# Order of transposes and matmuls on TensorE in the attention of a graph network's encoder

## The chip, the cores and the metric

One core of a Trainium2 chip. The metric is the device time of one execution in microseconds (us); less is better. The kernel runs four graph layers one after the other; the change lies in one stage of the fourth.

## The reference, cut to what matters

There are 2708 nodes with 512 features and a dense adjacency matrix. The stage in question is the attention of the fourth layer's encoder, with four heads of 128 features:

```
Xw  = einsum('hnd,hde->hne', Xh, W)                  # 4 heads x 2708 x 128
sig = sigmoid(f1[:, :, None] + f2[:, None, :])
att = masked_softmax(pattern * sig, pattern != 0)    # both patterns are adj
Xa  = einsum('hij,hjd->hid', att, Xw)
Xn  = batchnorm(Xa as 2708 x 512); then an MLP, and a decoder that uses att again
```

## The kernel before, in words

Rows are padded to 22 tiles of 128. The stage works in **units**: unit u is one tile of 128 rows for one head. There are 88 units (`UNITS`); `place` (L1116) gives each its row tile, head and side r, so that units 2n and 2n+1 are the two row tiles of the same head. Such a pair is called pair n here (44 of them); one output of the attention is made for each pair.

What a unit goes through, and on which engine:

- `score(u)` (L1214, ScalarE): sigmoid of a 128x2708 row block into the buffer `slot(u)` (L1220). There are five such buffers; before it overwrites one, it waits until all transposes of the unit that used it last are done (`before`, L1124: four units back for three of four units, else eight).
- `weigh(u)` (L1267, VectorE): product with the adjacency rows and the row maximum (L1273).
- GpSimd: the negated maximum `nm` (L1203).
- `expo(u)` (L1223, ScalarE): exp with row sums, in place (L1225). Its end lets the transposes of unit u begin (`p_ready`).
- `turn_group(u, g)` (L1334, TensorE): 22 transposes in six groups g = 0 to 5 (four tiles each, two in the last), each group into one of five PSUM banks that are used in turn (`ring`, L1113). Each transpose is one instruction at L1342. Group 0 waits for `p_ready`; every group waits until the group five places earlier was copied out.
- the copies of the groups to SBUF tile `pt`: group 2 on ScalarE (`keep`, L1228, row L1232), the others on VectorE (`keep`, L1276, row L1281). `kept` (L1128) gives the semaphore and its count.
- `mul(n, lo, hi)` (L1346, TensorE): of the 22 accumulating matmuls of pair n those from lo to hi; the moving operand is the pair's copied transposes, 256 columns. Each of these matmuls is two instructions at L1354 in the trace.

TensorE's loop (L1366 to L1376) runs over the units and in each over the six groups: the transposes of group g of unit u, then a part of the matmuls of the pair before, n = u//2 - 1. The 11 matmuls that a unit does are spread over its groups as 1, 2, 2, 2, 2, 2. Pair 43 has its matmuls behind the loop (L1376).

ScalarE's order is written out by hand for four units b to b+3 (L1242 to L1262): `expo(b)`, `keep(b-1)`, `expo(b+1)`, `expo(b+2)`, `keep(b)`, `expo(b+3)`, `score(b+4)`, `keep(b+1)`, `score(b+5)`, `score(b+6)`, `keep(b+2)`, `score(b+7)`. A table load stands at each change between exp and sigmoid. Every eighth unit a small row of inverse sums is handled besides (`ri_out`, `inverse`, `turn_ri`).

VectorE copies the groups of unit u in order (all but group 2); behind its group 4 stands `weigh(u+3)`, behind group 0 of an even unit the copy of a finished accumulator, `raw` (L1283).

SyncE stores each copied group of a pair to HBM (L1170). GpSimd also fetches adjacency rows and scales finished outputs (L1195).

Of the kernel before, what the change touches and what calls it, by code (L numbers as in the profile page):

```python
# [49 lines left out]
def wait(eng, sem, value):  # L50

    if isinstance(value, int) and value <= 0:
        return
    eng.wait_ge(sem, value)
# [24 lines left out]
def build(nc, x, adj_rows, adj_cols, adj_tiles, ident, w0, a0_self, a0_neigh, b0, w1, b1, w2a, w2b, a2_w, a2_b,  # L79
# [30 lines left out]
    with top:  # L110
# [87 lines left out]
        with ExitStack() as ph:  # L198
# [15 lines left out]
            with nc.Block() as block:  # L214
                @block.sync
                def _(sp):
                    sp.dma_start(w0_sb[:, :, :], w0).then_inc(w_in, 16)
                    sp.dma_start(vecs[0], a0_self.partition_broadcast(128)).then_inc(vec_in, 16)
                    sp.dma_start(vecs[1], a0_neigh.partition_broadcast(128)).then_inc(vec_in, 16)
                    sp.dma_start(idt[:, :], ident).then_inc(vec_in, 16)  # L220

                    def body(i):
                        for q in (0, 1):
                            j = 2 * i + q
                            wait(sp, turned, j - 1)
                            sp.dma_start(xin[q][:, :], x[j]).then_inc(x_in[q], 16)
                            wait(sp, mask_done, j - 1)
                            sp.dma_start(al[q][:, :], adj_cols[j]).then_inc(adj_in[q], 16)
                    pair_loop(sp, body, first=True)
# [582 lines left out]

        with ExitStack() as ph:
            R, xn, st, xin, xt, _, w_sb = norm_buffers(ph)
            rows = [sb(ph, f"rows{q}", [P, NP]) for q in (0, 1)]
            pr = [sb(ph, f"pr{q}", [P, NP]) for q in (0, 1)]
# [275 lines left out]
        with ExitStack() as ph:  # L1092
# [27 lines left out]
            def slot(u):  # L1120

                return v[u % 4 if u % 4 < 3 else 3 + (u // 4) % 2]
# [5 lines left out]
            def kept(g_index):  # L1128

                u, g = divmod(g_index, NG)  # L1130
                if g == ACT_GROUP:
                    return kept_act, u + 1
                return kept_dve, u * (NG - 1) + g + 1 - int(g > ACT_GROUP)
# [14 lines left out]
            with nc.Block() as block:  # L1148
# [183 lines left out]
                @block.tensor  # L1332
                def _(pe):
                    def turn_group(u, g):  # L1334
                        a, b = GROUPS[g]
                        index = NG * u + g
                        if g == 0:
                            pe.wait_ge(p_ready, u + 1)
                        if index >= len(ring):
                            pe.wait_ge(*kept(index - len(ring)))  # L1340
                        for m in range(a, b):
                            t = pe.transpose(ring[index % len(ring)][:, (m - a) * P:(m - a + 1) * P],  # L1342
                                             slot(u)[:, m * P:(m + 1) * P], idt[:, :])
                        t.then_inc(t_grp, 1)

                    def mul(n, lo, hi):  # L1346
                        h = n % H3
                        for m in range(lo, hi):
                            if m == 0 and n >= 2:
                                pe.wait_ge(xr_ready, n - 1)  # L1350
                            if m % 4 == 0 or m == lo:
                                for r in (0, 1):
                                    pe.wait_ge(*kept(NG * (2 * n + r) + m // 4))
                            t = pe.matmul(acc_t[n % 2][:, 0:P2], HA[:, m, h * D3:(h + 1) * D3],  # L1354
                                          pt[n % 2][:, m, :, :].rearrange("p r n -> p (r n)"),
                                          start=(m == 0), stop=(m == T - 1))
                        if hi == T:
                            t.then_inc(m_done, 1)

                    def turn_ri(p):  # L1360
                        pe.wait_ge(ri_ready, p + 1)
                        wait(pe, ri_row, p)
                        pe.transpose(small[0:2 * H3, 0:P], ri[:, :], idt[:, :]).then_inc(ri_turned, 1)

                    pe.wait_ge(pad_zero, len(v))
                    for u in range(UNITS):  # L1366
                        for g in range(NG):
                            turn_group(u, g)
                            if u == 2 and g == 0:
                                pe.wait_ge(ha_in, 16)  # L1370
                            if u >= 2:
                                base = 11 * (u % 2)
                                mul(u // 2 - 1, base + 11 * g // NG, base + 11 * (g + 1) // NG)
                        if u % 8 == 0 and u > 0:
                            turn_ri(u // 8 - 1)
                    mul(HEADS - 1, 0, T)  # L1376
                    turn_ri(PAIRS - 1)
# [416 lines left out]
```

## Time and profile before

| | |
|---|---|
| Three runs, us | 3789.41, 3787.44, 3789.86 (median 3789.41) |
| Profiled execution, its own time | 3787.66 us |
| Its span from first to last instruction | 3786.1 us |
| TensorE busy over the span | 3400.1 us (90%) |
| VectorE / ScalarE busy | 2330.3 us (62%) / 1679.4 us (44%) |
| Stage of the change | transposes L1342 from 2349.5 us, last matmul L1354 begins 3053.2 us |

Times in the rows are microseconds from the span's start. A busy TensorE includes the modelled ends of pipelined matmuls, so the distance between two starts is the better measure of what an instruction costs it. In a row of a timeline "[1.02 <-ACT pt L1232]" means that the engine had been idle for 1.02 us before this instruction and that the row of ScalarE named there released it. PE is TensorE, PEld its weight loads, DVE VectorE, ACT ScalarE, POOL GpSimd.

### The profile page before, as it was taken

To read this page: it belongs to the slowest core of one execution; us is meant where nothing else is said; L and a number is where in the kernel's file an instruction comes from. 1 tells how busy PE (TensorE), PEld (TensorE's weight loads), DVE (VectorE), ACT (ScalarE), POOL (GpSimd) and SP (SyncE) were. 2 spreads that over 40 slices of the span, in tenths; PEclk is the share of its full clock that TensorE was granted. 3 is DMA by queue.
4 is the path that set the end of the run, shared out by engine and by line. 5 is a ranking of instruction groups with operands and counts; after the bars stand their busy time and mean duration, and the time that the engine had idled before them with its cause. 6 is when DMAs were issued, how large, how long until landed. Compare 5 with 4: busy or idle time off the path is not lost. (4 is left out here: it accounts for less than half of the span.)

```text
span 3786.1 us, 39785 instructions
## 1 busy us (share of the span) xinstructions
PE 3400.1 (90%) x13931; PEld 2134.0 (56%) x13931; DVE 2330.3 (62%) x2850; ACT 1679.4 (44%) x1527; POOL 271.1 (7%) x459
## 2 busy tenths in 40 slices
PE   7899999999978899995999995999999967999995
PEld 4433333333323677773555553877777735888884
DVE  4488888988966455555555553777777734122226
ACT  1288888888852111112222223777777702000002
POOL 1000000000002011110000001000010000000003
PEclk9999999999999999997999997999999989999997
DMA  7500000000012455553222224666666630866653
GB/s 284 179 16 8 15 8 15 16 8 15 8 44 91 189 222 229 218 215 137 79 87 94 94 79 175 233 243 244 244 243 245 231 141 15 369 272 269 273 219 123
DMA packets 109759, 557.51 MB, mean 147 GB/s; under 512 B 14320, under 2 KB 20432, under 8 KB 85584
## 3 DMA queue, kind: packets, MB, share of 16 engines
q1 hardware_dynamic: 88592, 432.35, 30.7%
q0 software_dynamic: 21056, 123.65, 8.5%
q8 instruction: 73, 1.20, 0.1%
q14 instruction: 38, 0.31, 0.0%
HBM read 363.77 MB, written 192.18 MB: 147 GB/s over the span
## 5 line engine op out<-in xcount | busy, mean ns | idle before, releaser
L528 PE MATMUL bank<-dist,hf 128*65 128x512 f32 (+1 forms) x2112 | 860.7, 561 | 63.3 <-ACT dist L491 63.3
L528 PEld LDWEIGHTS bank<-dist,hf 128*65 128x65 f32 x2112 | 277.4, 138 | 637.7 <-issue 489.3
L1354 PE MATMUL bank<-pt,HA 128*128 128x256 f32 x1936 | 505.1, 381 | 3.0 <-DMA HA<-features 3.0
L491 ACT ACTIVATE dist<-dist 128x1408 f32<-128x1408 f32 x352 | 469.2, 1368 | 1.5
L1543 PE MATMUL bank<-w,EM 128*128 128x256 f32 x1936 | 427.0, 381 | 12.7 <-DMA w<-weights 12.7
L993 PE MATMUL bank<-HB,pt 128*128 128x512 f32 x968 | 436.7, 593 | 0.0
L1543 PEld LDWEIGHTS bank<-w,EM 128*128 128x128 f32 x1936 | 369.7, 191 | 63.6 <-DMA w<-weights 12.9
L422 DVE TENSOR_TENSOR dist<-msk,sB 128x1408 f32<-128x1408 uint8 x208 | 337.0, 1620 | 74.7 <-PE bank L528 68.5
L1342 PE MATMUL bank<-idt,v 128*128 128x128 f32 x1936 | 304.4, 278 | 79.5 <-ACT pt L1232 50.7
L482 ACT ACTIVATE dist<-dist,neg_t 128x1408 f32<-128x1408 f32 x208 | 305.2, 1467 | 151.9 <-DVE dist L422 151.9
L1354 PEld LDWEIGHTS bank<-pt,HA 128*128 128x128 f32 x1936 | 328.6, 191 | 26.8 <-DMA HA<-features 3.4
L1281 DVE COPY pt<-bank 128x512 f32<-128x512 f32 (+1 forms) x440 | 265.4, 631 | 105.6 <-PE bank L1342 104.4
L1342 PEld LDWEIGHTS bank<-idt,v 128*128 128x128 f32 x1936 | 242.8, 143 | 149.2 <-ACT pt L1232 67.4
L1273 DVE CUSTOM_DVE_ANT_0 v<-v,rows 128x2708 f32<-128x2708 f32 x88 | 261.4, 2971 | 70.0 <-ACT v L1220 54.7
L164 PE MATMUL bank<-w_sb,xt 128*128 128x512 f32 x528 | 252.6, 622 | 24.4 <-DVE HL L599 11.2
L425 DVE SCALAR_TENSOR_TENSOR dist<-msk,neg_t,sB 128x1408 f32<-128x1408 uint8 x144 | 257.7, 1789 | 24.6 <-PE bank L528 22.0
L993 PEld LDWEIGHTS bank<-HB,pt 128*128 128x128 f32 x968 | 174.2, 191 | 170.2 <-issue 170.2
L146 ACT ACTIVATE xt<-bank 128x512 f32<-128x512 f32 x88 | 52.5, 597 | 484.0 <-PE bank L140 483.2
L1220 ACT ACTIVATE v<-fB,f 128x2708 f32<-128x2708 f32 x88 | 224.1, 2549 | 78.9 <-PE bank L1342 70.9
L1225 ACT ACTIVATE v<-v,nm 128x2708 f32<-128x2708 f32 x88 | 224.1, 2549 | 74.4 <-POOL nm L1203 74.1
L1600 DVE TENSOR_TENSOR at<-bank,riB 128x256 f32<-128x256 f32 x44 | 18.7, 425 | 327.9 <-PE bank L1543 327.9
L699 PE MATMUL bank<-HR,hi 128*128 128x512 f32 x484 | 201.8, 417 | 18.0 <-ACT hi L790 18.0
(161 smaller groups left out, 3684.9 us busy)
## 6 DMA issues: line engine op xcount, KB each, us to landing
w<-weights SPq DMA_DIRECT2D x44, 2816.0 KB, 9.9
weights<-pt SPq DMA_DIRECT2D x220, 512.0 KB, 3.8
al<-in_adj_cols SPq DMA_DIRECT2D x22, 1408.0 KB, 7.5
at<-in_adj_tiles SPq DMA_DIRECT2D x22, 1408.0 KB, 6.7
rows<-in_adj_rows SPq DMA_DIRECT2D x22, 1408.0 KB, 6.8
mrow<-in_adj_rows POOLq DMA_DIRECT2D x22, 1354.0 KB, 8.3
rows_low<-mrow POOLq DMA_DIRECT2D x22, 1354.0 KB, 5.1
rows<-rows_low POOLq DMA_DIRECT2D x22, 1354.0 KB, 8.5
```

Source lines behind the costliest of these rows:

```text
L164: t = pe.matmul(pj[0:P, :], xt[:, k, :], w[:, k, :], start=(k == 0), stop=(k == KT - 1))
L422: dve.tensor_tensor(d[:, :], msk[:, m, c * CW:(c + 1) * CW], sB[hh][:, :], ALU.add).then_inc(d_ready, 1)
L425: dve.scalar_tensor_tensor(out=d[:, :], in0=msk[:, m, c * CW:(c + 1) * CW], scalar=neg_t[0:P, m, bass.ds(hp * 2 + hh, 1)], in1=sB[hh][:, : ...
L482: act.activation(d[:, :], d[:, :], ACT.Square, bias=neg_t[0:P, m, bass.ds(hp * 2 + hh, 1)]).then_inc(sq_act, 1)
L491: act.activation(d[:, :], d[:, :], ACT.Exp, scale=-1.0).then_inc(p_ready, 1)
L528: mm = pe.matmul(sums_bank(hh, k)[0:FW, 0:(b - a) * P], hf[hh][:, m, :], d[:, a * P:b * P], start=(m == 0), stop=(m == T - 1))
L993: t = pe.matmul(acc[q][0:P, :], pt[q][:, m, :], HB[0:P, m, :], start=(m == 0), stop=(m == T - 1))
L1273: dve.tensor_tensor_reduce(s[:, 0:N], s[:, 0:N], rows[r][:, :], 1.0, LOW, ALU.mult, ALU.max, mx[:, u % 16:u % 16 + 1]).then_inc(mx_ready, 1)
L1281: dve.tensor_copy(dst, src).then_inc(kept_dve, 1)
L1342: t = pe.transpose(ring[index % len(ring)][:, (m - a) * P:(m - a + 1) * P], slot(u)[:, m * P:(m + 1) * P], idt[:, :])
L1354: t = pe.matmul(acc_t[n % 2][:, 0:P2], HA[:, m, h * D3:(h + 1) * D3], pt[n % 2][:, m, :, :].rearrange("p r n -> p (r n)"), start=(m == 0), ...
L1543: t = pe.matmul(acc_t[n % 2][:, 0:P2], EM[:, m, h * D3:(h + 1) * D3], w[k][:, m, :], start=(m == 0), stop=(m == T - 1))
```

## The change

In each group TensorE does the part of the previous pair's matmuls first and the transposes of the current unit behind them. The wait for the features (`ha_in`) at unit 2, group 0 moves with the matmuls, and so stands ahead of that group's transposes. Nothing else is altered; the instructions are the same ones.

```diff
                     for u in range(UNITS):
                         for g in range(NG):
-                            turn_group(u, g)
                             if u == 2 and g == 0:
                                 pe.wait_ge(ha_in, 16)
                             if u >= 2:
                                 base = 11 * (u % 2)
                                 mul(u // 2 - 1, base + 11 * g // NG, base + 11 * (g + 1) // NG)
+                            turn_group(u, g)
                         if u % 8 == 0 and u > 0:
                             turn_ri(u // 8 - 1)
                     mul(HEADS - 1, 0, T)
```

## Rows read from the trace of the kernel before

**Rows 1.** The page's first line: the span of the profiled execution.
```profile
span 3786.1 us, 39785 instructions
```

**Rows 2.** Busy time by stretch: start:end, length, then engines, TensorE clock, DMA share, GB/s.
```profile
2356.30:2369.60 13.30, 9.58 (x37) 8.43 (x38) 8.45 (x12) 10.09 (x9) 0.42 (x2) 0.50 1.04 399
...
2380.00:3040.00 660.00, 613.01 (x3701) 524.15 (x3700) 511.16 (x686) 511.56 (x384) 51.69 (x112) 1.00 0.64 242
```

**Rows 3.** Who waited for whom, 2380 to 3040: total us, times, longest us.
```profile
ACT v L1225 <- POOL nm L1203: 71.5, 21, 3.4
ACT v L1220 <- PE bank L1342: 64.4, 20, 3.3
...
PE bank L1342 <- ACT pt L1232: 47.0, 40, 1.4
...
PEld bank L1342 <- ACT v L1225: 6.1, 21, 0.3
```

**Rows 4.** Timeline of TensorE's matmuls, 2700 to 2740: start, us, what.
```profile
2703.95 0.60 PE L1342 MATMUL bank<-idt,v 128*128 128x128 f32 x4
...
2715.55 0.66 PE L1342 MATMUL bank<-idt,v 128*128 128x128 f32 x4 [1.02 <-ACT pt L1232]
...
2720.82 0.38 PE L1342 MATMUL bank<-idt,v 128*128 128x128 f32 x2
...
2730.73 0.66 PE L1342 MATMUL bank<-idt,v 128*128 128x128 f32 x4
2731.22 0.60 PE L1354 MATMUL bank<-pt,HA 128*128 128x256 f32 x2
2731.66 0.60 PE L1342 MATMUL bank<-idt,v 128*128 128x128 f32 x4
2732.09 1.03 PE L1354 MATMUL bank<-pt,HA 128*128 128x256 f32 x4
...
2735.57 0.60 PE L1342 MATMUL bank<-idt,v 128*128 128x128 f32 x4
```

**Rows 5.** Timeline of VectorE and GpSimd in the same stretch.
```profile
2704.59 0.69 DVE L1281 COPY pt<-bank 128x512 f32<-128x512 f32 x1 [0.61 <-PE bank L1342]
...
2705.19 2.97 DVE L1273 CUSTOM_DVE_ANT_0 v<-v,rows 128x2708 f32<-128x2708 f32 x1
...
2708.26 0.21 POOL L1203 TENSOR_SCALAR nm<-mx 128x1 f32<-128x1 f32 x1 [4.15 <-DVE mx L1273]
```

**Rows 6.** Timeline of ScalarE in the same stretch.
```profile
2708.51 2.55 ACT L1225 ACTIVATE v<-v,nm 128x2708 f32<-128x2708 f32 x1 [3.41 <-POOL nm L1203]
...
2714.92 0.58 ACT L1232 ACTIVATE pt<-bank 128x512 f32<-128x512 f32 x1
...
2721.24 2.55 ACT L1220 ACTIVATE v<-fB,f 128x2708 f32<-128x2708 f32 x1 [3.29 <-PE bank L1342]
...
2723.70 0.58 ACT L1232 ACTIVATE pt<-bank 128x512 f32<-128x512 f32 x1
...
2728.03 2.56 ACT L1225 ACTIVATE v<-v,nm 128x2708 f32<-128x2708 f32 x1
...
2730.49 0.19 ACT L1225 ACTIVATION_READ_ACCUMULATOR v<-v,nm 128x1 f32 x1
```

**Rows 7.** Weight loads of the first transposes of units 4 and 48.
```profile
2382.99 0.42 PEld L1342 LDWEIGHTS bank<-idt,v 128*128 128x128 f32 x4 [0.29 <-ACT v L1225]
...
2730.73 0.42 PEld L1342 LDWEIGHTS bank<-idt,v 128*128 128x128 f32 x4 [0.29 <-ACT v L1225]
```

**Rows 8.** Timeline of TensorE in unit 2, behind the wait for the features.
```profile
2364.98 1.22 PE L1354 MATMUL bank<-pt,HA 128*128 128x256 f32 x2 [2.98 <-DMA HA<-features]
2365.99 1.06 PE L1342 MATMUL bank<-idt,v 128*128 128x128 f32 x4
...
2373.09 0.38 PE L1342 MATMUL bank<-idt,v 128*128 128x128 f32 x2
```

**Rows 9.** Timeline of TensorE near the stage's end: first transposes of unit 84.
```profile
3015.21 0.66 PE L1342 MATMUL bank<-idt,v 128*128 128x128 f32 x4
```

## The prediction

> **What bounds the stage now.** Write T(u,g) for the transposes of group g of unit u and M(u,g) for the matmuls that unit u does in that group: one for g = 0, two for g = 1 to 5.
>
> I began with the busy table by stretch. Over 660 us in the middle of the stage TensorE is busy 613 us, VectorE and ScalarE 511 us each, at a granted clock of 1.00 [rows 2]. TensorE looks like the bound, but the busy table cannot say whether its gaps are paid for. So next the waits of the same stretch [rows 3]: TensorE waits 40 times, 47.0 us in all, for ScalarE's copy of a group (L1232). But ScalarE waits too: 20 times 3.2 us for TensorE's transposes before a sigmoid, 21 times 3.4 us for the maximum before an exp. When all engines wait for each other, a loop of dependences sets the pace, and one must walk it. Its fourth kind of wait is easily missed: 21 times a weight load of a transpose waits 0.3 us for an exp (L1225).
>
> The timelines give the loop, here for units 44 to 48. T(44,4) starts at 2703.95 [rows 4]. VectorE had waited 0.61 us for it, copies it at 2704.59, does weigh(47) at 2705.19; GpSimd negates the maximum at 2708.26 [rows 5]; ScalarE, idle for 3.41 us, starts expo(47) at 2708.51. Then follow table load and score(48), and at 2714.92 keep(45), the copy of group 2 [rows 6]. Its bank is the one that T(46,1) needs: TensorE, idle for 1.02 us, starts T(46,1) at 2715.55 and comes to T(46,5) at 2720.82 [rows 4]. ScalarE had waited 3.29 us for that: score(50) at 2721.24, keep(46), score(51), table load, expo(48) at 2728.03, whose read of the sums begins at 2730.49 and takes 0.19, so ends 2730.68 [rows 6]. That releases T(48,0) at 2730.73: its weight load shows 0.29 us of idle time put down to this exp [rows 7]. TensorE goes on to T(48,4) at 2735.57 [rows 4], and the loop is closed.
>
> Its four legs, start to start:
> - T(44,4) to T(46,1), over VectorE, GpSimd and ScalarE: 11.60 us
> - T(46,1) to T(46,5), TensorE alone: 5.27 us
> - T(46,5) to T(48,0), ScalarE: 9.91 us
> - T(48,0) to T(48,4), TensorE alone: 4.84 us
>
> The sum is 31.62 us for four units. The period, from T(4,0) at 2382.99 [rows 7] to T(84,0) at 3015.21 [rows 9], is 632.22/20 = 31.61 us. The loop accounts for all of it, with waits at each of the four handovers. So only these legs count, and TensorE's other wait, T(47,1) for keep(46), is beside the loop: by that branch TensorE is ready for T(48,0) at about the moment of its release, as its matmul row there shows no idle time [rows 4] while the weight load does [rows 7]. The branch has no reserve, but isn't later.
>
> **The prices.** From 2731.22 to 2731.66 M(48,0) takes 0.44 us, from 2731.66 to 2732.09 four transposes take 0.43 us, and (2735.57 - 2731.66)/3 = 1.303 us for a group of T and M leaves 0.87 us for an M of two matmuls [rows 4]. An M(u,0) is thus 0.43 us shorter than the others. That is the whole of the matter.
>
> **What moves.** The sequence T0 M0 T1 M1 ... T5 M5 becomes M0 T0 M1 T1 ... M5 T5. Nothing is added or removed; what can change is only how many matmuls lie between two transposes that begin or end a leg. From T(.,g) to a later T(.,h) the old order holds the Ms from g up to the one before h, the new one those behind g up to h itself: it drops M(g) and takes in M(h). So:
> - T(46,1) to T(46,5): M1 is dropped, M5 taken in, both of 0.87 us. No change.
> - T(48,0) to T(48,4): M0 (0.44) is dropped, M4 (0.87) taken in. **+0.43 us**, 4.84 becomes 5.27.
> - The two legs over other engines hold no matmul that they wait for. No change.
> - T(47,1) to T(48,0), the branch: M1 dropped, M0 taken in, -0.43 us. TensorE is early at T(48,0) and waits there: its time is set by expo(48), not by this branch. The gain is lost in that wait.
>
> So the period grows from 31.61 to 32.04 us. The gaps at T(.,1) remain as they are, 1.02 and 1.39 us: the part put ahead of the wait (M1, 0.87 us) is matched by a part that was ahead of it before (the M of the group that the leg starts from). This is what makes the change look better than it is.
>
> **New waits.** M(2,0) with its wait for the features now stands ahead of T(2,0), which was done in the 2.98 us of that wait [rows 8]. Queued behind it are T(2,0) and all that copies it. M(2,0) still starts at 2364.98; T(2,0) takes the place of T(2,1) at 2365.99, T(2,1) that of T(2,2), and so on at the half clock of the start (0.50, so 1.2 GHz, [rows 2]) and then at the full one. T(2,5) is behind one more T and one more M of two. After M(2,2) it is as before, at 2370.48 in the old sequence (the sum of 2373.09 less two groups of 1.303), and then T, M, T, M, T, M at full clock, 3 x 1.303 = 3.9 us, gives 2374.38 in place of 2373.09 [rows 8]: **+1.29 us**. ScalarE's score(6) waits for T(2,5), as score(50) does in the loop, so T(4,0) comes 1.29 us later.
>
> The matmuls' own waits move ahead of a T as well. M(u,0) of an even unit waits for group 0 of unit u-1 to be copied; T(u-1,5) already waited for that same copy, since it takes that bank. It also waits for `raw` of two pairs ago, which VectorE does two units earlier. M(u,2) and M(u,4) need groups 1 and 2 of unit u-1, for which T(u,0) and T(u,1), still ahead of them, have waited. All free. VectorE's `raw` waits for M(u-1,5), now earlier: free. SyncE's stores and GpSimd's loads follow the same copies, up to 0.43 us later in a period: hidden, as nothing in rows 3 waits for a DMA. The small transpose every eighth unit still has its input in time: it lies behind T(.,5) as before.
>
> **The end.** From T(84,0) on no sigmoid or exp is left in the loop and TensorE runs to its last matmul. There M(84,0) is already done: -0.43 us.
>
> **Sum.** +1.29 + 20 x 0.434 - 0.43 = +9.5 us (0.434 is 5.27 less 4.84 before rounding). On the profiled execution, 3787.66 us with a span of 3786.1 [rows 1], this makes 3797.2 us; the median of the runs is 1.75 us above that execution, so 3798.9 us, 0.25% more than 3789.41. A measurement of this kernel can tell about 0.2%, 7.6 us, from no change.
>
> Bounds of what the trace does not show: the start can go with another moment of the clock's rise. If it came behind T(2,5) instead of near 2369.8, the 3.3 us of work until 2373.09 would take twice as long, +3.3 us; if the 4.6 us from 2364.98 at 0.50 ran at full clock, -2.3 us. I take neither, since TensorE's work from 2365.0 on is as dense as before. Leg 4 lies between +0.37 per period (if the 0.49 us that T(48,0) takes behind its wait, 0.06 more than T(48,1) takes, fell to 0.43) and +0.44: 8.3 to 9.7 us in all. Forecast alone: 3794 to 3803 us.
>
> **Rivals.**
> - Faster: the gaps are filled. If keep(45) and keep(46) came at times of ScalarE's own, M1 would be done inside the gaps at T(46,1) and T(47,1): 40 gaps [rows 3] x 0.87 = -34.8 us, 3754.6 us. It decides whether ScalarE is free-running. Against it: ScalarE's two long waits in each period, 3.29 and 3.41 us [rows 6], both end with a TensorE transpose, one directly, one over VectorE, and those transposes move behind one more M. Busy shares (613 of 660 us, [rows 2]) speak for it. The Trainium skill, "Perfetto Trace Analysis", section "Identifying the Most-Contended Engine", says to take the engine with the highest occupancy first, and its "Optimization Strategy" takes a gap repeated on it as a hint at too few buffers for the next tile; by that this change, which gives TensorE work ahead of its bank waits, would bring this rival's gain. The loop says otherwise: the gap is a bank wait, but of a loop through TensorE itself. Chance 0.06.
> - No change: T(4k,0) has reserve against expo(4k), so that +0.43 is absorbed; it decides at a reserve of 0.43 us. 3789 us, or up to 3794 if part of it. For it: the matmul row shows no idle time at 2730.73. Against it: the weight load waited 0.29 us, 21 times. Chance 0.11.
> - Slower still: the longer wait at T(4k,0) brings the clock down, or the start costs the +3.3: 3802 us and above. The clock was 1.00 with gaps of 1.4 us, longer than the 0.5 expected there. Chance 0.06.
>
> The forecast has 0.77. The range that holds 8 in 10 takes in the forecast's own and the no-change case: 3789 to 3803. Slower by over 0.2% (above 3797.0) is most of the forecast, 0.67, and the slower rival: 0.72. Within 0.2%: the no-change rival and the forecast's lower edge, 0.22. Faster: 0.06.
>
> **What would show it.** The waits: weight loads for ScalarE's exp, 21 times, from 0.3 to about 0.7 us each; a matmul row at T(4k,0) with some 0.4 us of idle time; TensorE's 40 waits at T(.,1) unchanged at 0.9 to 1.4 us. T(4,0) to T(84,0) 640.9 us. T(2,5) at 2374.4; the last matmul of the stage 9.5 us later. Wrong if the gaps at T(.,1) shrink towards 0.1 to 0.5 us with the period below 31.6 (first rival), or if the period stays at 31.61.

## The result and the profile after

The changed kernel takes 3799.83 us in the median of 8 runs, the kernel before 3787.43 us in 8: a ratio of 1.0032, 95% interval 1.0021 to 1.0042. A second series of 11 runs of the changed kernel (`after_again` below) gave 3797.32 against 3787.66 us, 1.0026 (1.0017 to 1.0035). It is slower, by 10 to 12 us; forecast were 9.5.

The busy table of the changed kernel, same stretch as [rows 2], shows only that TensorE is 7 us less busy:

```profile
2380.00:3040.00 660.00, 605.93 (x3642) 515.42 (x3643) 505.44 (x675) 513.98 (x382) 51.83 (x112) 1.00 0.63 238
```

The waits of the same stretch say where, beside [rows 3] (total us, times, longest us):

```profile
ACT v L1225 <- POOL nm L1203: 80.5, 21, 3.8
PEld bank L1342 <- ACT pt L1232: 64.8, 41, 1.8
ACT v L1220 <- PE bank L1342: 64.3, 20, 3.3
...
PE bank L1342 <- ACT pt L1232: 48.4, 41, 1.4
PEld bank L1342 <- ACT v L1225: 15.2, 21, 0.7
PE bank L1342 <- ACT v L1225: 6.8, 21, 0.3
```

TensorE's gaps for ScalarE's copies, the ones that one would expect to be filled, are as they were: 41 for 48.4 us, against 40 for 47.0 (one more falls into the stretch). ScalarE waits for TensorE as before a sigmoid, 3.2 us each. Two kinds of wait have grown by 0.4 us each: the weight load for the exp, 0.7 us in place of 0.3, now with a gap of 0.3 us between matmuls too, and ScalarE's wait for the maximum, 3.8 in place of 3.4.

TensorE's timeline over one period, to be read beside [rows 4]:

```profile
2707.21 0.66 PE L1342 MATMUL bank<-idt,v 128*128 128x128 f32 x4 [0.32 <-ACT v L1225]
2707.70 1.03 PE L1354 MATMUL bank<-pt,HA 128*128 128x256 f32 x4
2708.57 0.60 PE L1342 MATMUL bank<-idt,v 128*128 128x128 f32 x4
...
2712.48 0.60 PE L1342 MATMUL bank<-idt,v 128*128 128x128 f32 x4
...
2724.09 0.65 PE L1342 MATMUL bank<-idt,v 128*128 128x128 f32 x4 [1.02 <-ACT pt L1232]
...
2729.35 0.38 PE L1342 MATMUL bank<-idt,v 128*128 128x128 f32 x2
...
2732.86 0.66 PE L1342 MATMUL bank<-idt,v 128*128 128x128 f32 x4 [1.37 <-ACT pt L1232]
...
2739.27 0.66 PE L1342 MATMUL bank<-idt,v 128*128 128x128 f32 x4 [0.33 <-ACT v L1225]
```

This is T(44,0) to T(48,0). The legs: T(44,0) at 2707.21 to T(44,4) at 2712.48 is 5.27 us, 4.84 before. Behind T(44,0) stand the four instructions of M1 (2707.70), where the two of M0 stood. T(44,4) to T(46,1) at 2724.09 is 11.61 us (11.60), T(46,1) to T(46,5) at 2729.35 is 5.26 (5.27), T(46,5) to T(48,0) 9.92 (9.91). One leg has grown by one matmul, three are unchanged; the period is 32.06 us.

The ends of the stage, in the timelines of weight loads and matmuls:

```profile
2367.07 1.22 PE L1354 MATMUL bank<-pt,HA 128*128 128x256 f32 x2 [4.11 <-DMA HA<-features]
...
2376.74 0.38 PE L1342 MATMUL bank<-idt,v 128*128 128x128 f32 x2
...
2386.66 0.42 PEld L1342 LDWEIGHTS bank<-idt,v 128*128 128x128 f32 x4 [0.72 <-ACT v L1225]
...
3027.74 0.42 PEld L1342 LDWEIGHTS bank<-idt,v 128*128 128x128 f32 x4 [0.72 <-ACT v L1225]
...
3065.52 0.27 PE L1363 MATMUL bank<-idt,ri 128*8 128x128 f32 x1
```

The last row is the small transpose behind the stage's last matmul; before, it started here:

```profile
3053.43 0.27 PE L1363 MATMUL bank<-idt,ri 128*8 128x128 f32 x1
```

| stretch | before | after | difference |
|---|---|---|---|
| first matmul (unit 2) to T(4,0) | 18.01 | 19.59 | +1.58 |
| T(4,0) to T(84,0), 20 periods | 632.22 | 641.08 | +8.86 |
| T(84,0) to the small transpose | 38.22 | 37.78 | -0.44 |
| sum in the stage | 688.45 | 698.45 | +10.00 |

The spans differ by 12.8 us. Of the rest, 2.09 us lie ahead of the first matmul (2364.98 against 2367.07) and 0.7 us behind the small transpose, where both kernels have the same instructions.

### The profile page after: what moved, and what is told of

Read it like the earlier page. It is cut to its first block and busy times, and to the rows that moved or that the text cites. A ratio compares the mean times of both kernels' runs of the same rounds, so it can differ in the third digit from the quotient of the medians.

```text
span 3798.9 us, 39785 instructions
## 1 busy us (share of the span) xinstructions
PE 3405.6 (90%) x13931; PEld 2135.1 (56%) x13931; DVE 2331.1 (61%) x2850; ACT 1681.3 (44%) x1527; POOL 272.2 (7%) x459
## 5 line engine op out<-in xcount | busy, mean ns | idle before, releaser
L1354 PE MATMUL bank<-pt,HA 128*128 128x256 f32 x1936 | 505.5, 381 | 4.1 <-DMA HA<-features 4.1
L1543 PEld LDWEIGHTS bank<-w,EM 128*128 128x128 f32 x1936 | 369.7, 191 | 63.6 <-DMA w<-weights 12.8
L1354 PEld LDWEIGHTS bank<-pt,HA 128*128 128x128 f32 x1936 | 328.7, 191 | 28.0 <-DMA HA<-features 4.3
L1281 DVE COPY pt<-bank 128x512 f32<-128x512 f32 (+1 forms) x440 | 266.1, 634 | 115.7 <-PE bank L1342 114.7
```

The source lines that it names most:

```text
L1281: dve.tensor_copy(dst, src).then_inc(kept_dve, 1)
L1543: t = pe.matmul(acc_t[n % 2][:, 0:P2], EM[:, m, h * D3:(h + 1) * D3], w[k][:, m, :], start=(m == 0), stop=(m == T - 1))
```

## The experiments

In all kernels only TensorE's loop was touched, and every one computes the whole reference. "The spread" is the number of matmuls that a unit does in its groups 0 to 5. Each was timed in turn with the kernel before on the same chip.

**1. The old order with the change's count in the leg** (`one_last_old`).

```diff
-                                mul(u // 2 - 1, base + 11 * g // NG, base + 11 * (g + 1) // NG)
+                                mul(u // 2 - 1, base + min(2 * g, 11), base + min(2 * g + 2, 11))
```

> The old order (transposes first), but the 11 matmuls of a unit are spread over its groups as 2, 2, 2, 2, 2, 1 in place of 1, 2, 2, 2, 2, 2. Loop theory (only the matmuls inside the two TensorE legs of the loop count, M(4k,0..3) and M(4k+2,1..4) in the old order): the leg T(4k,0) to T(4k,4) holds 8 matmuls in place of 7, so the period grows from 31.61 to 32.04 us and the time by 20 x 0.43 and 0.43 at the start, +9 us, as with the change, though no transpose has been moved. Rival (the new order itself costs, by what stands next to what on TensorE): no change, within 2 us of before.

Measured: 3795.81 us against 3788.05, ratio 1.0021 (1.0012 to 1.0030). The period is 32.05 us, from T(44,0), the first row, to T(48,0), the last; T(46,1) and T(47,1) stand between them:

```profile
2702.84 0.65 PE L1342 MATMUL bank<-idt,v 128*128 128x128 f32 x4 [0.32 <-ACT v L1225]
...
2719.71 0.66 PE L1342 MATMUL bank<-idt,v 128*128 128x128 f32 x4 [1.02 <-ACT pt L1232]
2728.48 0.66 PE L1342 MATMUL bank<-idt,v 128*128 128x128 f32 x4 [1.37 <-ACT pt L1232]
2734.89 0.66 PE L1342 MATMUL bank<-idt,v 128*128 128x128 f32 x4 [0.32 <-ACT v L1225]
```

These are the gaps and distances of the changed kernel, without its order. One more matmul behind T(4k,0) is enough to make the loss.

**2. The new order with that matmul taken back** (`one_last_new`): the edit of experiment 1 on top of the change.

> The new order (matmuls first) with the spread 2, 2, 2, 2, 2, 1. Loop theory: the leg T(4k,0) to T(4k,4) holds M1 to M4, 8 matmuls, but the leg T(4k+2,1) to T(4k+2,5) holds M2 to M5, 7 in place of 8; the period is 31.61 us again and the time that of before, +0.4 us. Rival (the new order itself costs): slower by 9 to 12 us, like the change.

Measured: 3786.92 us against 3788.05, ratio 0.9999 (0.9990 to 1.0008). The rows for T(4,0) and T(84,0):

```profile
2384.39 0.42 PEld L1342 LDWEIGHTS bank<-idt,v 128*128 128x128 f32 x4 [0.73 <-ACT v L1225]
...
3017.61 0.42 PEld L1342 LDWEIGHTS bank<-idt,v 128*128 128x128 f32 x4 [0.72 <-ACT v L1225]
```

That is 633.22/20 = 31.66 us a period. All 88 units have the new order, and no loss shows in the whole time: its interval reaches from 0.1% faster to 0.1% slower. The stage by itself takes 2.0 us longer than before, where 0.4 were expected: 1.8 at the start, 1.0 over the 20 periods, -0.9 at the end. The 0.05 us above 31.61 is a wait that I had not expected: in every second period T(4k+2,5), such as T(46,5), comes 0.1 us late, its weight load released by a copy of VectorE's. The weight load at T(4k,0) waits 0.7 us here too, as in the slower kernel: the length of that wait says nothing about the time.

**3. The new order in every fourth unit only** (`only_4k`).

```diff
-                            turn_group(u, g)
+                            if not (u % 4 == 0):
+                                turn_group(u, g)
...
+                            if u % 4 == 0:
+                                turn_group(u, g)
```

> The new order in every fourth unit only (u % 4 == 0), the old one in the other three. Loop theory: the leg T(4k,0) to T(4k,4) gains 0.43 us as in the whole change, and besides M(4k,0) now stands between T(4k-1,1) and T(4k,0) with M1 to M5 of the old order before it, 11 matmuls in place of 10, so that TensorE comes late to T(4k,0) by some 0.38 us: the period grows by 0.75 to 0.8 us to 32.4 and the time by 15 to 17 us, more than with the whole change. The wait of T(4k,0) for the exp is gone. Rival (each moved group costs its share): a quarter of the change, +3 us.

Measured: 3804.22 us against 3788.05, +16.2 us, ratio 1.0043 (1.0029 to 1.0056). The rows are T(43,1), T(46,1) and T(47,1); the first and the last, a period apart, are 32.37 us from each other:

```profile
2702.45 0.66 PE L1342 MATMUL bank<-idt,v 128*128 128x128 f32 x4 [1.39 <-ACT pt L1232]
2726.05 0.66 PE L1342 MATMUL bank<-idt,v 128*128 128x128 f32 x4 [1.89 <-ACT pt L1232]
2734.82 0.66 PE L1342 MATMUL bank<-idt,v 128*128 128x128 f32 x4 [1.39 <-ACT pt L1232]
```

A quarter of the edit costs more than all of it. No wait for the exp is left; the chain now runs over T(4k-1,1), and the gap at T(46,1) has grown from 1.0 to 1.9 us, since what lies ahead of it on the other engines takes as long as before while TensorE has less to do in between.

**4. The new order in the other three units** (`all_but_4k`): the same edit with `u % 4 != 0`.

> The new order in three of four units, the old one where u % 4 == 0. Loop theory: the leg from T(4k,0) holds M0 to M3 again, 7 matmuls, the leg from T(4k+2,1) 8: period 31.61, time +1.3 us (the start alone). The gaps at T(4k+2,1) shrink from 1.0 to about 0.15 us, as two more matmuls lie ahead of them, and the period doesn't change by that. Rival (each moved group costs its share): three quarters of the change, +9 us. Rival (filled gaps are time won): faster by 20 x 0.87 = 17 us.

Measured: 3786.49 us against 3788.05, ratio 0.9995 (0.9986 to 1.0004). The rows are T(44,0), T(46,1), T(47,1) and T(48,0):

```profile
2701.00 0.66 PE L1342 MATMUL bank<-idt,v 128*128 128x128 f32 x4 [0.75 <-ACT v L1225]
2717.45 0.66 PE L1342 MATMUL bank<-idt,v 128*128 128x128 f32 x4 [0.16 <-ACT pt L1232]
2726.22 0.66 PE L1342 MATMUL bank<-idt,v 128*128 128x128 f32 x4 [1.38 <-ACT pt L1232]
2732.62 0.66 PE L1342 MATMUL bank<-idt,v 128*128 128x128 f32 x4 [0.75 <-ACT v L1225]
```

This is the clearest case against reading gaps: the one at T(46,1) is filled, 0.16 us in place of 1.02. The period stays at 31.62 us, and what the gap lost came back as a longer one at T(48,0), 0.75 us. Work was moved from one gap to another.

**5. The changed kernel again** (`after_again`), unaltered.

> The changed kernel once more, unaltered, to narrow its interval. In the first pair of profiles 10.0 us of the difference lies in the stage and 2.1 us ahead of its first transpose, where both kernels have the same instructions. Loop theory: the stage's part is there again (period 32.05 us), +9.5 to 10 us, and what lies ahead of the stage varies from one execution to the next, so that the ratio comes out nearer to 1.0026 than to 1.0032. Rival (the change also costs time ahead of the stage): +12 us again, with a first transpose 2 us later than in the kernels of the last batch.

Measured: 3797.32 us against 3787.66, ratio 1.0026 (1.0017 to 1.0035). Its first matmul, T(4,0), T(84,0) and small transpose:

```profile
2363.24 1.22 PE L1354 MATMUL bank<-pt,HA 128*128 128x256 f32 x2 [3.50 <-DMA HA<-features]
...
2382.51 0.42 PEld L1342 LDWEIGHTS bank<-idt,v 128*128 128x128 f32 x4 [0.72 <-ACT v L1225]
...
3023.35 0.42 PEld L1342 LDWEIGHTS bank<-idt,v 128*128 128x128 f32 x4 [0.72 <-ACT v L1225]
...
3061.14 0.27 PE L1363 MATMUL bank<-idt,ri 128*8 128x128 f32 x1
```

The stage takes 697.90 us, 9.45 more than before (19.27, 640.84, 37.79 by the parts of the table above). Its first matmul comes 3.83 us earlier than in the first profile of the same kernel. So what lies ahead of the stage varies by more than the 2.09 us in question, and those are no part of the change. In the profiles of experiments 1 to 4, 6 and 7 it comes between 2363.39 and 2366.60, in that of experiment 8 at 2362.95.

**6. One matmul out of each leg** (`three_last`). With the old order; the wait for `ha_in` moves into `mul`, ahead of the first matmul.

```diff
+                    SPREAD = ((1, 1, 2, 2, 2, 3),) * 4
...
-                                base = 11 * (u % 2)
-                                mul(u // 2 - 1, base + 11 * g // NG, base + 11 * (g + 1) // NG)
+                                lo = sum(SPREAD[u % 4][:g]) + 11 * (u % 2)
+                                mul(u // 2 - 1, lo, lo + SPREAD[u % 4][g])
```

> The old order with the matmuls of every unit spread as 1, 1, 2, 2, 2, 3: one matmul leaves group 1 for group 5, which lies in neither TensorE leg of the loop. Loop theory: both legs hold one matmul less (6 for 7 and 7 for 8), the period falls by 2 x 0.43 or a little more to 30.6 to 30.75 us, the time by 17 to 18 us; the gap at T(4k+2,1) shrinks from 1.0 to some 0.6 us or stays, it pays nothing by itself. Rival (TensorE's total work and its number of waits decide): no change, within 2 us.

Measured: 3769.83 us against 3787.66, -17.8 us, ratio 0.9950 (0.9937 to 0.9963). The rows are T(14,1), T(15,1), T(18,1), T(19,1) and T(22,1):

```profile
2462.13 0.65 PE L1344 MATMUL bank<-idt,v 128*128 128x128 f32 x4 [0.59 <-ACT pt L1232]
2470.58 0.66 PE L1344 MATMUL bank<-idt,v 128*128 128x128 f32 x4 [0.96 <-ACT pt L1232]
2492.98 0.66 PE L1344 MATMUL bank<-idt,v 128*128 128x128 f32 x4 [0.47 <-ACT pt L1232]
2501.32 0.66 PE L1344 MATMUL bank<-idt,v 128*128 128x128 f32 x4 [0.96 <-ACT pt L1232]
2523.73 0.66 PE L1344 MATMUL bank<-idt,v 128*128 128x128 f32 x4 [0.58 <-ACT pt L1232]
```

Two periods from 2462.13 to 2523.73, 30.80 us each: 0.81 less, of 0.87 for two matmuls. The range of 30.6 to 30.75 us was missed by 0.05, and the stage got shorter by 16.2 us, not by the whole time's 17.8. The wait of experiment 2 is here again, a weight load of T(4k+2,5) held 0.29 us by a copy of VectorE's in every second period. The loop theory holds in the other direction too, less what that wait takes.

**7. More of them out** (`legs_lighter`): the same code with `SPREAD = ((1, 1, 1, 2, 3, 3), (1, 2, 2, 2, 2, 2), (1, 1, 1, 1, 2, 5), (1, 2, 2, 2, 2, 2))`.

> The old order with spreads of their own for units 4k (1, 1, 1, 2, 3, 3) and 4k+2 (1, 1, 1, 1, 2, 5), the other two as before. Loop theory: the leg from T(4k,0) holds 5 matmuls for 7, the leg from T(4k+2,1) 5 for 8. That is 5 x 0.43 = 2.2 us less in a period, if no other loop takes over; TensorE's two gaps (1.0 and 1.4 us) shrink to a few tenths. Period 29.4 to 29.8 us, time -35 to -45 us. Rival (gaps are waits for ScalarE, which is busy three quarters of the time and can't go faster): no more than -18 us.

Measured: 3751.89 us against 3787.66, -35.8 us, ratio 0.9906 (0.9892 to 0.9920), at the small end of what was expected; the stage by itself got shorter by 32.4 us, and the period missed its range. The pattern repeats every eight units, 60.14 us, so 30.07 us for four, not 29.4 to 29.8:

```profile
2575.77 0.66 PE L1344 MATMUL bank<-idt,v 128*128 128x128 f32 x4 [0.16 <-ACT pt L1232]
2578.75 0.66 PE L1344 MATMUL bank<-idt,v 128*128 128x128 f32 x4 [0.16 <-DVE pt L1281]
2580.66 0.44 PE L1344 MATMUL bank<-idt,v 128*128 128x128 f32 x2 [0.38 <-DVE pt L1281]
2635.91 0.66 PE L1344 MATMUL bank<-idt,v 128*128 128x128 f32 x4 [0.15 <-ACT pt L1232]
```

The rows are T(30,1), T(30,4), T(30,5) and, eight units on, T(38,1). A new releaser is there: VectorE's copies (L1281), which are named in no gap of the kernel before. The bank of T(30,4) is that of T(29,5), whose copy stands on VectorE behind weigh(32), and that waits for the sigmoid of unit 32:

```profile
2575.37 2.98 DVE L1273 CUSTOM_DVE_ANT_0 v<-v,rows 128x2708 f32<-128x2708 f32 x1 [1.85 <-ACT v L1220]
...
2578.28 0.42 DVE L1281 COPY pt<-bank 128x256 f32<-128x256 f32 x1
```

The copy ends at 2578.70 and T(30,4) starts at 2578.75. With only one matmul in each group ahead of it TensorE comes to T(4k+2,4) before its bank is free, so matmuls taken out ahead of that point no longer shorten the period. I read the missed range as the cost of these waits; no run was made on that alone.

**8. The legs nearly empty** (`legs_empty`): the same with `SPREAD = ((1, 0, 0, 0, 5, 5), (2, 2, 1, 2, 2, 2), (0, 1, 1, 1, 2, 6), (1, 1, 0, 1, 4, 4))`.

> The old order with the matmuls of the units 4k to 4k+3 spread as (1, 0, 0, 0, 5, 5), (2, 2, 1, 2, 2, 2), (0, 1, 1, 1, 2, 6), (1, 1, 0, 1, 4, 4): the legs hold 1 and 5 matmuls for 7 and 8, and the branch through T(4k+3,1) holds less before T(4k,0). Loop theory: the loop is now shorter than TensorE's own work in four units, 88 transposes at 0.109 and 44 matmuls at 0.434 us, 28.65 us; TensorE runs without gaps, the period is 28.65 to 29 us, the time -55 to -60 us, 3730 us. Rival (VectorE's copies, which come in bursts now, hold up the banks): period above 29.5 us, as with the lighter spread.

Measured: 3728.69 us against 3787.66, -59.0 us, ratio 0.9847 (0.9835 to 0.9860). The busy table over 600 us of the stage, and two of the small transposes, eight units apart:

```profile
2380.00:2980.00 600.00, 600.00 (x3682) 528.46 (x3680) 507.08 (x683) 507.74 (x380) 51.14 (x110) 1.00 0.69 266
```

```profile
2702.55 0.27 PE L1367 MATMUL bank<-idt,ri 128*8 128x128 f32 x1
...
2760.17 0.27 PE L1367 MATMUL bank<-idt,ri 128*8 128x128 f32 x1
```

TensorE's matmul rows show no gap at all; the period is 57.62/2 = 28.81 us, close to the 28.65 us that were counted as TensorE's own work (28.69 with the prices as they are printed there). Short waits are left on the weight loads, 7.2 us in 600, and none of them is for ScalarE's copies any more:

```profile
PEld bank L1344 <- ACT v L1225: 3.6, 20, 0.2
PEld bank L1344 <- DVE pt L1281: 3.6, 9, 0.4
```

The rival that banks would hold the period above 29.5 us is out for this spread. It beats both kernels, with the same transposes and matmuls in another order.

## Why the prediction was right, point by point

**The loop.** The prediction's four legs made up the measured period of before, and of the four only T(4k,0) to T(4k,4) changed, 4.84 to 5.27 us, as written. Experiments 1 to 4 show that this count is the cause: the loss is there with the old order and that count, it is gone with the new order and the old total in the two legs (8 and 7 for 7 and 8), it grows to 16.2 us when only the units 4k are turned, and it is gone when they alone are not. A cost of the new order as such would have given 0, 9, 3 and 9 us in these four; measured were +7.8, -1.1, +16.2 and -1.6 us. The stage alone, from its first matmul L1354 to the small transpose L1363, is free of what varies ahead of it and behind it, and follows the loop's count within 0.4 us but for the second kernel:

| kernel | stage, us | against 688.45 before | expected by the loop |
|---|---|---|---|
| one_last_old | 697.60 | +9.15 | +9 |
| one_last_new | 690.42 | +1.97 | +0.4 |
| only_4k | 705.38 | +16.93 | +15 to +17 |
| all_but_4k | 690.14 | +1.69 | +1.3 |

Experiment 3 also bears out what the prediction said of the branch from T(4k-1,1) to T(4k,0), that it has no reserve: one matmul more on it, and it set the pace.

**The sum.** +1.29 at the start was +1.58 in one profile and +1.26 in the other. The difference is the moment of the clock's rise, which the bounds left open. Behind the wait for the features all three traces have the same instructions: matmul, four transposes, two matmuls, four transposes, two matmuls, four transposes. The third group of transposes behind the wait starts here, in the kernel before, the changed kernel and its second profile:

```profile
2370.48 0.60 PE L1342 MATMUL bank<-idt,v 128*128 128x128 f32 x4
...
2372.84 0.60 PE L1342 MATMUL bank<-idt,v 128*128 128x128 f32 x4
...
2368.69 0.60 PE L1342 MATMUL bank<-idt,v 128*128 128x128 f32 x4
```

From the first matmul (2364.98, 2367.07, 2363.24) that is 5.50, 5.77 and 5.45 us: +0.27 and -0.05, which is what the start was off from +1.29 within 0.02 us. In the first profile of the changed kernel the clock was at its lower level (1.2 GHz) until 2372.40 at least, 5.3 us behind the first matmul; in the trace of before the lower level is shown until 2369.80, 4.8 us behind it, and in the second profile until about 2368.0, 4.7 us behind it. Why it rose later in one of them, no run shows. The busy table of the changed kernel at the start of unit 2:

```profile
2367.10:2372.40 5.30, 5.30 (x17) 4.37 (x18) 3.79 (x5) 2.10 (x1) 0.21 (x1) 0.50 1.02 416
2372.60:2380.00 7.40, 6.26 (x38) 5.16 (x36) 4.61 (x6) 2.84 (x2) 0.21 (x1) 1.00 0.03 10
```

20 x 0.434 = 8.7 was 8.86 and 8.62; -0.43 at the end was -0.44 and -0.43. The stage's +9.5 was +10.0 and +9.45. The median moved by 12.4 us in the first series and 9.7 in the second; the forecast's ratio, 1.0025, lies in both intervals. That the forecast time, 3798.9 us, came within 1 us of the measured 3799.83 is luck in part: it set out from a median of three runs that lies 2.0 us above that of eight, and the median of the first series moved by 2.9 us more than forecast. The stage is what the prediction can claim.

**The rivals.** The filled gaps: T(.,1) kept 0.9 to 1.4 us, and experiment 4, which does fill one of them, gained nothing that can be measured. The prediction put filled gaps at -34.8 us. The gaps belong to a loop through TensorE itself: the waits for ScalarE's copies were gone in experiment 8 with the same five banks. The Trainium skill, "Perfetto Trace Analysis", section "Optimization Strategy", says of a repeated gap that it can mean too few buffers. No run here had more than five banks, so whether a sixth would have opened the loop as well is not shown; what is shown is that work put into a gap gained nothing and work taken out of the legs did. The reserve at T(4k,0): none, the full 0.43 us appeared. The clock stayed at 1.00 through the steady part, so the slower rival had no part either.

**What was imprecise.** I expected a gap of 0.4 us between matmuls at T(4k,0); it shows as 0.32, with 0.72 on the weight load. The weight load is the row to read there. In experiment 7 my range for the period was too low by 0.3 us, as I had not walked the loop over VectorE's copies; waits for the same engine's copies stand in the traces of experiments 2 and 6, where the period was 0.05 us above what was expected. And two sums of chances are off by 0.01: 0.67 and 0.06 make 0.73, not 0.72, and 0.11 and 0.10 make 0.21, not 0.22.

## What to carry to other kernels

Where engines wait for each other in turn, gaps on the busiest one are not free room. Find the loop whose legs sum to the period, and count the work inside its legs; moving work from one gap to another gained nothing here, and an order that puts one longer piece into a leg costs its length once per round. The same count shows what to move out: here the position of the matmuls, without a change to any of them, was worth 59 us. And read the weight loads as well as the matmuls: the handover that sets the pace here, 0.29 us at T(48,0), stands only there.

## What the runs showed that I had not expected

Turning a quarter of the units cost 16.2 us where turning all cost 9.7 to 12.4. And the time ahead of the stage differs from one execution to the next by up to 3.8 us (first matmul of the stage at 2363.24 and 2367.07 in two executions of the same kernel), which is as much as a tenth of a per cent: for an effect of 0.3% the stretch between two fixed rows of the stage is a sharper measure than the whole time.
